# Where a routed expert layer begins: one-hots choice by choice, gather indices taken from the list itself, and a quarter of tile 0's gate and up ahead of tile 1's rows

## The chip, the core and the metric

The kernel runs on one core of a Trainium2 chip. The metric is the device time in microseconds of one execution, from the first to the last instruction and what lies around them; lower is better. The core has five engines with queues of their own: TensorE (PE), VectorE (DVE), ScalarE (ACT), GpSimd (POOL) and SyncE (SP), and 16 DMA engines which serve the transfers that any of them issue.

## The reference, cut to what matters

Eight sequences of 512 tokens with 512 features go through a cross attention (16 heads), are normalised, and then through a mixture of 8 experts, of which each token takes two:

```python
x = x + xattn(layernorm(x), ctx, ctx, Wq, bq, Wk, bk, Wv, bv, Wo, bo)
flat = layernorm(x).reshape(T, H)                       # T = 4096, H = 512
scores = softmax(flat @ router_weight.T + router_bias)  # 8 experts
topk_vals, topk_idx = top_k(scores, 2)
w = zeros((T, E)).at[arange(T)[:, None], topk_idx].set(topk_vals)
gu = einsum('th,ehf->tef', flat, gate_up_proj) + gate_up_bias      # 2 x 512 columns
gate, up = minimum(gu[..., :I], 7), clip(gu[..., I:], -7, 7)
down = einsum('tei,eih->teh', (up + 1) * gate * sigmoid(1.702 * gate), down_proj) + down_bias
x = x + einsum('teh,te->th', down, w)
```

## The kernel before

The program has three stages, each a block of its own, and at a block's end all five engines meet in a barrier before any of them starts on the next one.

**Attention** (`attention_stage`) works through 32 units of one sequence and four heads. A hand-written list `ORDER` gives every engine its work. At its end the last tokens get their router logits, and from them the best two experts (`hot[0]`, `hot[1]`; `hots` is both), their rank among the tokens of that expert (`place`), and their softmax weight (`share`). Tokens are handled in groups of 128-token tiles; groups 7 and 8 are the last five tiles. After `share` SP stores the weights behind the rows of the normalised input: row r of `xln_dram` holds 512 features and 8 weights. The store counts on the semaphore `w_stored`.

**Routing** (`routing_stage`) makes the work list. The experts' loads are cut into 39 tiles of 256 tokens. DVE works out each tile's expert (`tile_expert`, `tile_changed`); these two, marked "tiles", are what SP waits for before `first_loads`, which issues the weights of the first two tiles: twice 2 MB for gate and up (`raw_g`) and 1 MB for down (`raw_d`). The places of the first 27 tiles of tokens were written to DRAM earlier (`token_list`); those of the last five are put in by matmuls with one-hots: `at_hot` (place within a column, 128 wide) and `col_hot` (column of the list, 78 wide) for both choices s, into `list_ps`, and then the earlier list is added by `choose`. The result is `token_of`, 78 columns of 128 token numbers, two columns a tile.

**Experts** (`expert_stage`) handles the 39 tiles. For each tile POOL gathers 2 x 128 rows by indirect DMA (`fetch`), PE transposes them into `t_ps` (`turn_rows`), ACT and DVE split the result into a high and a low part (`row_hi`, `row_lo`), PE does gate and up in four parts f (`gate_up`, 24 matmuls a part, three passes of high and low), ACT and DVE the activation, PE the down product, and the sum goes back into `out` by gather, add and scatter. The weights are split into high and low in the same way, when a tile's expert differs from that of two tiles before (`gate_up_hi`, `gate_up_lo`). `fetch(0)` waits for all weight stores:

```python
e.wait_ge(w_stored, 16 * weights_stored)
fetch(0)
fetch(1)
fetch_sums(0)
```

Of the kernel before, what the change touches and what calls it, by code (L numbers as in the profile page):

```python
# [5 lines left out]
ALU = mybir.AluOpType  # L6
# [8 lines left out]
P = 128  # L15
# [53 lines left out]
def attention_stage(nc, x, ctx_t, w_t, bq, bk, bv, bo, router_wt, router_b, out, xln_dram, w_rows, w_stored, token_list, listed, route, ident):  # L69
# [8 lines left out]
    iota, token, base, before, ones_b, hot, ranks = (route[n] for n in ("iota", "token", "base", "before", "ones_b", "hot", "ranks"))  # L78

# [5 lines left out]

    weights_of = lambda g: slots_of(g) if g < groups[-1] else slice(SLOTS, SLOTS + 2)

    with ExitStack() as ctx:
# [54 lines left out]
        hots = sb("hots", [P, SLOTS, E], BF16)  # L143
        expo = sb("expo", [P, SLOTS, E])
        weight = sb("weight", [P, SLOTS + 2, E])
        exp_sum = sb("exp_sum", [P, SLOTS])
        inv_sum = sb("inv_sum", [P, SLOTS])
# [17 lines left out]
        def step(s):  # L165
# [537 lines left out]
        def on_dve(e):  # L703
# [136 lines left out]
            def share(g):  # L840
                slots, n = slots_of(g), GROUPS[g][1]
                e.wait_ge(softened.sem, softened[g])
                if g in groups[1:-1]:
                    e.wait_ge(w_stored, 16 * g)
                then(e.tensor_reduce(exp_sum[:, slots], expo[:, slots, :], AX.X, ALU.add))
                then(e.tensor_tensor(weight[:, weights_of(g), :], expo[:, slots, :], hots[:, slots, :], ALU.mult))
# [3 lines left out]
                e.tensor_tensor(weight[:, weights_of(g), :], weight[:, weights_of(g), :], inv_sum[:, slots].unsqueeze(2).to_broadcast([P, n, E]),  # L850
# [149 lines left out]
        def on_sp(e):  # L1000
# [63 lines left out]
            for kind, *what in ORDER:  # L1064
# [16 lines left out]
                elif kind == "share":  # L1081
                    g, = what
                    e.wait_ge(weight_made.sem, weight_made[g])
                    e.dma_start(w_rows[:, tiles_of(g), :], weight[:, weights_of(g), :]).then_inc(w_stored, 16)
# [12 lines left out]
def routing_stage(nc, route, token_list, listed, tile_hot, tile_expert, tile_changed, token_of, n_tiles, groups, first_loads):  # L1097
# [12 lines left out]
    KT = TOP_K * left  # L1110

    with ExitStack() as ctx:
# [11 lines left out]
        expert_f = sb("expert_f", [P, n_tiles])  # L1124
        changed_f = sb("changed_f", [P, n_tiles])
# [15 lines left out]
        at_hot = sb("at_hot", [P, KT, P])  # L1141
# [22 lines left out]
        def on_dve(e):  # L1164
# [8 lines left out]
            def last():  # L1173
# [23 lines left out]
            then(e.tensor_tensor(tile_hot[:, :, 0, :], iota[:, 0:E].unsqueeze(1).to_broadcast([P, n_tiles, E]),  # L1197
                                 expert_f[:, :].unsqueeze(2).to_broadcast([P, n_tiles, E]), ALU.is_equal))
# [649 lines left out]
```

## Time and profile before

| | |
|---|---|
| median of 3 runs | 1750.2 us (1749.93 to 1752.56) |
| the profiled execution, its own time | 1748.89 us |
| its span in the trace | 1747.2 us |
| mean granted TensorE clock | 0.969 of 2.4 GHz |
| TensorE matmuls busy | 1621.0 us, 93% of the span |
| TensorE weight loads busy | 1189.2 us, 68% |
| VectorE / ScalarE / GpSimd busy | 1278.3 / 659.2 / 856.5 us |

The profiled execution's own time is 1.69 us above its span, for what lies around the instructions. A busy share is a mean over the whole span: attention ends at about 990 us, routing runs from there to about 1010 us, and the experts take the rest. Times in the rows below are microseconds from the span's start.

### The profile page before, as it was taken

What the parts mean: (1) busy time and instruction counts of PE and PEld (TensorE: products, weight loads), DVE (VectorE), ACT (ScalarE), POOL (GpSimd) and SP (SyncE); (2) the same over time, 40 slices, a digit from 0 to 9 for tenths busy, and PEclk for the clock granted to TensorE, in tenths of its full rate; (3) what the DMA queues carried; (4) which work ended last, traced back from release to release, by engine and by line L of the source; (5) the groups of instructions that cost most, each with busy time, mean ns of one, the idle gap of its engine ahead of it and who ended that gap; (6) DMA issues with size and microseconds to landing.
All of it is one profiled execution on the core that took longest, in us unless ns stands there. A gap on an engine that the chain in (4) does not pass through costs nothing. (4 is left out here: it accounts for less than half of the span.)

```text
span 1747.2 us, 30307 instructions
## 1 busy us (share of the span) xinstructions
PE 1621.0 (93%) x9614; PEld 1189.2 (68%) x9614; DVE 1278.3 (73%) x2426; ACT 659.2 (38%) x1273; POOL 856.5 (49%) x677
## 2 busy tenths in 40 slices
PE   5889999999999999999997479999999999999995
PEld 3555555555555555555543369999999998999994
DVE  3675777878778777787785567777878688777873
ACT  3354544545445445444442142223332233223320
POOL 4365656566666666666767223343333333334332
PEclk9999999999999999999999579999999999999998
DMA  6342332433433434343322442234453353324321
GB/s 216 84 121 68 107 110 81 122 92 94 119 96 94 120 79 135 85 112 80 92 67 38 104 167 74 86 98 159 164 170 92 99 199 119 101 84 154 98 86 60
DMA packets 101077, 188.99 MB, mean 108 GB/s; under 512 B 28208, under 2 KB 29616, under 8 KB 100912
## 3 DMA queue, kind: packets, MB, share of 16 engines
q1 hardware_dynamic: 79952, 124.25, 24.9%
q0 software_dynamic: 20960, 62.76, 11.3%
q8 instruction: 77, 1.26, 0.4%
q14 instruction: 88, 0.72, 0.2%
HBM read 204.32 MB, written 37.51 MB: 138 GB/s over the span
## 5 line engine op out<-in xcount | busy, mean ns | idle before, releaser
L769 DVE TENSOR_REDUCE negmax<-max_ps 128x2 f32<-128x1024 f32 x256 | 312.2, 1220 | 162.9 <-PE max_ps L526 162.4
L650 ACT ACTIVATE pt<-work 128x512 f32<-128x512 f32 x512 | 278.3, 594 | 249.6 <-PE work L538 234.9
L946 POOL TENSOR_TENSOR acc<-acc,pt 128x1024 f32<-128x1024 f32 x128 | 303.7, 2376 | 129.2 <-ACT pt L650 129.1
L1440 PE MATMUL gu_ps<-xgT_hi,wg_hi 128*128 128x256 f32 x1248 | 356.3, 285 | 0.0
L1440 PE MATMUL gu_ps<-xgT_hi,wg_lo 128*128 128x256 f32 x1248 | 352.7, 283 | 0.0
L1440 PE MATMUL gu_ps<-xgT_lo,wg_hi 128*128 128x256 f32 x1248 | 351.9, 282 | 0.0
L943 POOL TENSOR_TENSOR acc<-pt 128x1024 f32<-128x1024 f32 x64 | 153.1, 2394 | 197.7 <-PE work L558 129.6
L1701 POOL DMA_INDIRECT out<-acc,idx x78 | 77.3, 991 | 329.0 <-DVE acc L1595 323.1
L1440 PEld LDWEIGHTS gu_ps<-xgT_lo,wg_hi 128*128 128x128 f32 x1248 | 236.3, 189 | 0.1
L1440 PEld LDWEIGHTS gu_ps<-xgT_hi,wg_hi 128*128 128x128 f32 x1248 | 236.0, 189 | 0.1
L1440 PEld LDWEIGHTS gu_ps<-xgT_hi,wg_lo 128*128 128x128 f32 x1248 | 235.6, 189 | 0.0
L526 PE MATMUL max_ps<-ks,qs 96*128 96x512 f32 x512 | 200.5, 473 | 26.0 <-DVE negmax L769 12.7
L1507 ACT ACTIVATE sig<-gate 128x256 f32<-128x256 f32 x156 | 65.1, 418 | 341.5 <-DVE gate L1559 338.9
L538 PE MATMUL work<-qs,ks 98*128 98x512 f32 x512 | 169.2, 407 | 11.6 <-DVE q_lo L756 5.6
L526 PEld LDWEIGHTS max_ps<-ks,qs 96*128 96x128 f32 x512 | 88.6, 193 | 87.8 <-issue 54.1
L550 PE MATMUL o_ps<-pt,v 128*32 128x512 f32 x1024 | 138.3, 612 | 1.7 <-ACT pt L650 1.7
L1454 PE MATMUL d_ps<-wd_hi,hid_hi 128*128 128x512 f32 x312 | 124.9, 400 | 9.5 <-DVE acc L1592 7.8
L1696 POOL DMA_INDIRECT acc<-out,idx x78 | 80.8, 1036 | 102.8 <-DMA out<-acc,idx 90.5
L538 PEld LDWEIGHTS work<-qs,ks 98*128 98x128 f32 x512 | 96.9, 191 | 47.0 <-issue 11.7
L780 DVE RECIPROCAL inv<-inv 128x128 f32<-128x128 f32 x128 | 120.7, 943 | 7.5 <-issue 4.8
L493 PE MATMUL work<-xT,wq 128*128 128x512 f32 x256 | 126.0, 615 | 0.0
L1559 DVE TENSOR_SCALAR gate<-gu_ps,bg 128x256 f32<-128x256 f32 x156 | 75.4, 484 | 66.9 <-PE gu_ps L1440 56.3
(211 smaller groups left out, 2971.5 us busy)
## 6 DMA issues: line engine op xcount, KB each, us to landing
raw_g<-w_gate_up SPq DMA_DIRECT2D x39, 2048.0 KB
raw_d<-w_down SPq DMA_DIRECT2D x39, 1024.0 KB
ks<-k_hi SPq DMA_DIRECT2D x252, 64.0 KB
qs<-q_hi SPq DMA_DIRECT2D x252, 64.0 KB
bd<-b_down SPq DMA_DIRECT2D x39, 256.0 KB
x_in<-x SPq DMA_DIRECT2D x32, 256.0 KB, 3.2
ctxT_raw<-ctx_t SPq DMA_DIRECT2D x32, 256.0 KB, 4.0
x<-x SPq DMA_DIRECT2D x32, 256.0 KB, 2.9
```

The source lines that it names most:

```text
L493: ins = e.matmul(to[:, :], wq[:, k, cols], xT[:, k, :], start=(k == 0), stop=(k == C - 1))
L526: ins = e.matmul(max_ps[:, j, :], qs[i][0:3 * HD, h, t * P:(t + 1) * P], ks[i][0:3 * HD, h, :], start=True, stop=True)
L538: e.matmul(to[:, :], ks[i][0:3 * HD + 2, h, k * P:(k + 1) * P], qs[i][0:3 * HD + 2, h, :], start=True, stop=True).then_inc(exp_ready.sem, 1)
L550: ins = e.matmul(o_ps[u % 2][HD * h:HD * (h + 1), :], v[:, k, c * P + HD * h:c * P + HD * (h + 1)], pt[k % 2][:, h, :], start=(k == 0), st ...
L650: e.activation(pt[k % 2][:, h, :], in_work("exp", u, k, h)[:, :], ACT.Exp, scale=scale).then_inc(exped.sem, 1)
L769: e.tensor_reduce(negmax[:, u % 2, n:n + 2], max_ps[:, :, :], AX.X, ALU.max, negate=True).then_inc(maxed.sem, 1)
L780: e.reciprocal(inv[:, cols], inv[:, cols]).then_inc(inverted.sem, 1)
L943: e.tensor_tensor(acc[:, heads, :], pt[0][:, heads, :], pt[1][:, heads, :], ALU.add).then_inc(added.sem, 1)
L946: e.tensor_tensor(acc[:, heads, :], acc[:, heads, :], pt[k % 2][:, heads, :], ALU.add).then_inc(added.sem, 1)
L1440: ins = e.matmul(gu_ps[n % GU_BANKS][:, part, :], wg[s][pw][:, k, cols], xgT[s][px][:, k, :], start=(k == 0 and m == 0), stop=(k == KD - 1 ...
L1454: ins = e.matmul(d_ps[j][:, :], hid[s][px][:, k, j * P:(j + 1) * P], wd[s][pw][:, k, :], start=(k == 0 and m == 0), stop=(k == KF - 1 and ...
L1696: e.indirect_dma_start(out=acc[s][:, j, :], out_offset=None, in_=out_rows, in_offset=slot_rows(i, j)).then_inc(acc_in[s], 16)
```

## The change

It has four parts.

1. The weights (`share`) of the last two groups move out of attention: routing makes them in one go for the last five tiles (40 columns), between `choose` and `token_1` on DVE, and SP stores them with one DMA after `first_loads`. The `w_stored` count that `fetch(0)` waits for drops by one, since there is one store fewer.
2. In routing, the one-hot of the tiles' experts (`tile_hot`) moves from ahead of `tile_expert` to behind `choose`, and `at_hot` and `col_hot` are made for choice 0, multiplied, and then for choice 1, where before both were made at once.
3. The gathers and scatters of the experts take a column of `token_of` as index; the copy into `idx` and its semaphore are gone.
4. PE does part f = 0 of tile 0's gate and up before `turn_rows(1)`; ACT does `row_hi(1)` behind the down weights of tile 0 and half the gate and up weights of tile 1.

```diff
-                at(3, ("best", g + 1, 0), ("best", g + 1, 1), ("count", g + 1), ("soft", g + 1), ("rank", g + 1), ("share", g), ("place", g + 1), ("share", g + 1))
+                at(3, ("best", g + 1, 0), ("best", g + 1, 1), ("count", g + 1), ("soft", g + 1), ("rank", g + 1), ("place", g + 1))
...
+            for s in range(TOP_K):
+                then(e.tensor_tensor(at_hot[:, s, :, :], iota[:, :].unsqueeze(1).to_broadcast([P, left, P]),
+                                     at_f[:, s, :].unsqueeze(2).to_broadcast([P, left, P]), ALU.is_equal))
+                then(e.tensor_tensor(col_hot[:, s, :, :], iota[:, 0:SLOTS].unsqueeze(1).to_broadcast([P, left, SLOTS]),
+                                     col_f[:, s, :].unsqueeze(2).to_broadcast([P, left, SLOTS]), ALU.is_equal))
+                last()
+                then(e.tensor_tensor(col_hot[:, s, :, :], col_hot[:, s, :, :],
+                                     token[:, done_tiles:].unsqueeze(2).to_broadcast([P, left, SLOTS]), ALU.mult), ("late", s))
...
+            e.wait_ge(w_stored, 16 * (len(groups) - 2))
+            then(e.tensor_reduce(exp_sum[:, late], expo[:, late, :], AX.X, ALU.add))
+            then(e.tensor_tensor(weight[:, late, :], expo[:, late, :], hots[:, late, :], ALU.mult))
+            last()
+            then(e.reciprocal(inv_sum[:, late], exp_sum[:, late]))
+            last()
+            then(e.tensor_tensor(weight[:, late, :], weight[:, late, :], inv_sum[:, late].unsqueeze(2).to_broadcast([P, left, E]), ALU.mult), "weights")
             e.wait_ge(listed_late, 1)
...
             first_loads(e)
+            e.wait_ge(vec, at["weights"])
+            e.dma_start(w_rows[:, done_tiles:, :], route["weight"][:, late, :]).then_inc(w_stored, 16)
...
             turn_rows(0)
-            for i in range(-1, n_tiles):
+            gate_up(0, range(1))
+            turn_rows(1)
+            gate_up(0, range(1, KF))
+            for i in range(n_tiles):
...
-                e.tensor_copy(idx[i % IDX][:, :], token_of[:, place * SUB:(place + 1) * SUB]).then_inc(idx_made.sem, 1)
-                e.wait_ge(idx_made.sem, idx_made[i])
```

On SP, from the last stores of attention to the end of routing (`xln_dram<-weight` is a store of weights, 3, 2 or 5 tiles of 8 columns; `rows` is the earlier list). Before:

```order
L1046 DMA xln_dram<-x 128x512 [waits ln2_made] x2
L1084 DMA xln_dram<-weight 128x3x8 [waits weight_made]
L1084 DMA xln_dram<-weight 128x2x8 [waits weight_made]
L1089 UNCONDITIONAL_BRANCH [waits xln_stored2,x2_stored2,x2_stored1,xln_stored3,xln_stored1,x2_stored3,x2_stored0,xln_stored0]
L1316 UNCONDITIONAL_BRANCH [waits barrier_Pool_Activation_PE_DVE_SP_release]
L1308 DMA rows<-token_list 128x2x128 [waits listed]
...
L1325 DMA raw_d<-w_down 128x4x512
L1312 UNCONDITIONAL_BRANCH
```

and now:

```order
L1040 DMA xln_dram<-x 128x512 [waits ln2_made] x2
L1083 UNCONDITIONAL_BRANCH [waits xln_stored2,x2_stored2,x2_stored1,xln_stored3,xln_stored1,x2_stored3,x2_stored0,xln_stored0]
L1318 UNCONDITIONAL_BRANCH [waits barrier_Pool_Activation_PE_DVE_SP_release]
L1308 DMA rows<-token_list 128x2x128 [waits listed]
...
L1327 DMA raw_d<-w_down 128x4x512
L1312 DMA xln_dram<-weight 128x5x8 [waits tiles_vec]
L1314 UNCONDITIONAL_BRANCH
```

Two small stores have left the end of attention, and one stands behind the last of the four weight loads.

On POOL, at the start of the experts, before:

```order
L1682 COPY idx<-token_of 128x2 [waits w_stored]
L1685 DMA xg<-xln_dram,idx 128x520 [waits idx_made]
L1685 DMA xg<-xln_dram,idx 128x520
L1682 COPY idx<-token_of 128x2
L1685 DMA xg<-xln_dram,idx 128x520 [waits idx_made]
L1685 DMA xg<-xln_dram,idx 128x520
L1696 DMA acc<-out,idx 128x512 x2
L1682 COPY idx<-token_of 128x2 [waits w_made,turned]
```

and now:

```order
L1684 DMA xg<-xln_dram,token_of 128x520 [waits w_stored]
L1684 DMA xg<-xln_dram,token_of 128x520 x3
L1696 DMA acc<-out,token_of 128x512 x2
L1684 DMA xg<-xln_dram,token_of 128x520 [waits w_made,turned]
L1684 DMA xg<-xln_dram,token_of 128x520
L1684 DMA xg<-xln_dram,token_of 128x520 [waits w_made,turned]
```

The copies and the wait for them are gone; the first gather itself now waits for `w_stored`.

On PE, the first rows of the experts: transposes of tile 0 (`gathered0`), of tile 1 (`gathered1`) and the first matmuls of gate and up. Before:

```order
L1424 MATMUL t_ps<-ident,xg 128x128 [waits gathered0]
L1424 MATMUL t_ps<-ident,xg 128x128 x3
L1424 MATMUL t_ps<-ident,xg 128x128 [waits xgT_lo_made,gathered1]
L1424 MATMUL t_ps<-ident,xg 128x128 x3
L1424 MATMUL t_ps<-ident,xg 128x128 [waits xgT_lo_made,gathered1]
L1424 MATMUL t_ps<-ident,xg 128x128 x3
L1440 MATMUL gu_ps<-xgT_hi,wg_hi 128x256 [waits xgT_lo_made,wg_lo_made0]
```

and now:

```order
L1424 MATMUL t_ps<-ident,xg 128x128 [waits gathered0]
L1424 MATMUL t_ps<-ident,xg 128x128 x3
L1440 MATMUL gu_ps<-xgT_hi,wg_hi 128x256 [waits xgT_lo_made,wg_lo_made0]
L1440 MATMUL gu_ps<-xgT_lo,wg_hi 128x256
...
L1440 MATMUL gu_ps<-xgT_hi,wg_lo 128x256
L1424 MATMUL t_ps<-ident,xg 128x128 [waits xgT_lo_made,gathered1]
```

The 24 matmuls of part 0 stand ahead of the eight transposes of tile 1.

## Rows read from the trace of the kernel before

**Rows 1.** The page: shares of the chain that ended last, by engine

```profile
PE 38%; DVE 1%; issue 1%; DMA 1%; POOL 0%; ACT 0%; ACTq 0%; DVEq 0%; POOLq 0%
```

**Rows 2.** Waits of PE after 1023 us: total us, times, longest

```profile
PE d_ps L1454 <- DVE acc L1592: 7.8, 5, 2.7
PE d_ps L1454 <- DVE hid_lo L1574: 1.6, 1, 1.6
```

**Rows 3.** Timeline of PE where the experts start: start, length, work, idle before

```profile
1017.32 1.97 PE L1424 MATMUL t_ps<-ident,xg 128*128 128x128 f32 x8 [8.99 <-DMA xg<-xln_dram,idx]
1021.02 1.97 PE L1424 MATMUL t_ps<-ident,xg 128*128 128x128 f32 x8 [1.74 <-DMA xg<-xln_dram,idx]
1022.64 0.56 PE L1440 MATMUL gu_ps<-xgT_hi,wg_hi 128*128 128x256 f32 x1
```

**Rows 4.** Timeline of DVE where the experts start

```profile
1019.95 0.69 DVE L1551 TENSOR_TENSOR xgT_lo<-t_ps,xgT_hi 128x512 fp32r<-128x512 f32 x1 [0.16 <-ACT xgT_hi L1481]
...
1034.11 1.22 DVE L1405 TENSOR_TENSOR wg_lo<-raw_g,wg_hi 128x1024 fp32r<-128x1024 f32 x1
```

**Rows 5.** Timeline of POOL where the experts start

```profile
1010.53 0.18 POOL L1682 COPY idx<-token_of 128x2 int32<-128x2 int32 x1 [18.54 <-POOLq L1312]
1011.27 1.06 POOL L1685 DMA_INDIRECT xg<-xln_dram,idx  x1 [0.56 <-POOL idx L1682]
1012.63 1.02 POOL L1685 DMA_INDIRECT xg<-xln_dram,idx  x1 [0.31 <-issue]
...
1022.81 0.95 POOL L1685 DMA_INDIRECT xg<-xln_dram,idx  x1 [0.30 <-issue]
```

**Rows 6.** DMA queue totals, 995 to 1014.5 us: packets, MB, share

```profile
q1 hardware_dynamic: 2046, 6.19, 84.5%
```

**Rows 7.** DMA queue totals, 1014.75 to 1015 us

```profile
q0 software_dynamic: 15, 0.06, 67.0%
q1 hardware_dynamic: 93, 0.02, 41.6%
```

**Rows 8.** Timeline of SP: last stores of attention, list, first weight load

```profile
989.79 1.02 SPq L1084 DMA_DIRECT2D xln_dram<-weight  x2
991.55 0.36 SPq L1308 DMA_DIRECT2D rows<-token_list  x1
997.24 0.40 SPq L1325 DMA_DIRECT2D raw_g<-w_gate_up  x1
```

**Rows 9.** DMA issues, whole span: KB each, median us from issue to landing

```profile
xln_dram<-x SPq DMA_DIRECT2D x32, 256.0 KB, 3.3
...
qs<-m_hi SPq DMA_DIRECT2D x32, 8.0 KB, 1.8
...
bk_col<-bk SPq DMA_DIRECT2D x1, 2.0 KB, 10.3
```

**Rows 10.** Timeline of DVE at the end of attention

```profile
989.68 0.17 DVE L858 COPY ranks<-work 128x16 f32<-128x16 f32 x1
...
990.25 0.17 DVE L850 TENSOR_TENSOR weight<-weight,inv_sum 128x16 f32<-128x16 f32 x1
```

**Rows 11.** Timeline of DVE in routing

```profile
994.18 0.48 DVE L1197 TENSOR_TENSOR tile_hot<-iota_f,expert_f 128x312 bf16<-128x312 f32 x1
...
997.12 1.49 DVE L1228 TENSOR_TENSOR at_hot<-iota_f,at_f 128x1280 f32<-128x1280 f32 x1
998.53 0.96 DVE L1231 TENSOR_TENSOR col_hot<-iota_f,col_f 128x780 f32<-128x780 f32 x1
999.53 1.04 DVE L1235 TENSOR_TENSOR col_hot<-col_hot,consts 128x390 f32<-128x390 f32 x2
...
1005.60 0.24 DVE L1252 COPY token<-list_ps 128x78 f32<-128x78 f32 x1 [3.25 <-PE list_ps L1293]
```

**Rows 12.** Busy time by stretch: PE, PEld, DVE, ACT, POOL, PEclk, DMA share, GB/s

```profile
1024.00:1026.00 2.00, 2.00 (x12) 2.00 (x11) 0.00 (x0) 2.00 (x5) 0.00 (x0) 0.51 0.64 179
1026.00:1028.00 2.00, 2.00 (x18) 2.00 (x18) 1.22 (x2) 2.00 (x3) 0.00 (x0) 1.00 0.00 0
```

More of the change, by code:

```diff
@@ L78, in attention_stage @@
     iota, token, base, before, ones_b, hot, ranks = (route[n] for n in ("iota", "token", "base", "before", "ones_b", "hot", "ranks"))
+    expo, hots, weight, exp_sum, inv_sum = (route[n] for n in ("expo", "hots", "weight", "exp_sum", "inv_sum"))
     SLOTS = 2 * T
@@ L1249, in on_dve @@
                 then(e.tensor_scalar(choose[:, c, :], row_slot[:, :], number[:, 0:1], None, ALU.is_equal), "choose")
+            then(e.tensor_tensor(tile_hot[:, :, 0, :], iota[:, 0:E].unsqueeze(1).to_broadcast([P, n_tiles, E]),
+                                 expert_f[:, :].unsqueeze(2).to_broadcast([P, n_tiles, E]), ALU.is_equal))
+            expo, hots, weight, exp_sum, inv_sum = (route[n] for n in ("expo", "hots", "weight", "exp_sum", "inv_sum"))
+            e.wait_ge(w_stored, 16 * (len(groups) - 2))
[5 more added lines that the diff above has]
+            then(e.tensor_tensor(weight[:, late, :], weight[:, late, :], inv_sum[:, late].unsqueeze(2).to_broadcast([P, left, E]), ALU.mult), "weights")
             e.wait_ge(listed_late, 1)
@@ L1288, in on_pe @@
                 for t in range(left):
-                    e.matmul(list_ps[:, :], at_hot[:, s * left + t, :], col_hot[:, s, t, :], start=(s == 0 and t == 0), stop=False)
+                    e.matmul(list_ps[:, :], at_hot[:, s, t, :], col_hot[:, s, t, :], start=(s == 0 and t == 0), stop=False)
             e.wait_ge(rows_in, 16)
@@ L1360, in expert_stage @@
         bu1 = [sb(f"bu1{s}", [P, KF]) for s in range(2)]
-        idx = [sb(f"idx{s}", [P, SUB], I32) for s in range(IDX)]
         xg = [sb(f"xg{s}", [P, SUB, DX]) for s in range(2)]
@@ L1531, in on_act @@
                         gate_up_hi(1, k, changed)
+                    row_hi(1)
                 if i + 2 < n_tiles:
@@ L1687, in slot_rows @@
             def slot_rows(i, j):
-                return bass.IndirectOffsetOnAxis(ap=idx[i % IDX][:, j:j + 1].bitcast(U32), axis=0)
+                column = in_list(i, n_tiles) * SUB + j
+                return bass.IndirectOffsetOnAxis(ap=token_of[:, column:column + 1].bitcast(U32), axis=0)
             def fetch_sums(i):
@@ L1779, in build @@
         route["hot"] = [sb(f"hot{i}", [P, 2 * T, E]) for i in range(TOP_K)]
+        route["expo"] = sb("expo", [P, 2 * T, E])
+        route["hots"] = sb("hots", [P, 2 * T, E], BF16)
+        route["weight"] = sb("weight", [P, 2 * T, E])
+        route["exp_sum"] = sb("exp_sum", [P, 2 * T])
+        route["inv_sum"] = sb("inv_sum", [P, 2 * T])
         route["ranks"] = sb("ranks", [P, 2 * T, E])
@@ L1811, in build @@
         groups = route_groups(NT, T)
-        routing_stage(nc, route, token_list, listed, tile_hot, tile_expert, tile_changed, token_of, n_tiles, groups, first_loads)
-        expert_stage(nc, raw, s_raw, xln_dram, w_stored, len(groups), out, w_gate_up, w_down, b_gate_up, b_down, tile_hot, tile_expert, tile_changed, token_of, ident, n_tiles)
+        routing_stage(nc, route, w_rows, w_stored, token_list, listed, tile_hot, tile_expert, tile_changed, token_of, n_tiles, groups, first_loads)
+        expert_stage(nc, raw, s_raw, xln_dram, w_stored, len(groups) - 1, out, w_gate_up, w_down, b_gate_up, b_down, tile_hot, tile_expert, tile_changed, token_of, ident, n_tiles)
 _INS = ["x", "ctx_t", "wq_t", "bq", "wk_t", "bk", "wv_t", "bv", "wo_t", "bo", "router_wt", "router_b",
```

48 lines of the change are left out of this document (14 added, 34 removed).

## The prediction

> **What bounds the kernel now.** The chain of work that ended last comes first: 38% of the span is PE's (each line's share is of the pieces that could be followed back), and no other engine has more than 1% [rows 1]. After 1023 us PE is held only 7.8 + 1.6 us in all, by DVE [rows 2]. So from the first matmul of gate and up PE runs through, and anything done in the 39 expert tiles apart from PE's own work is hidden. What the change can move is the moment at which PE starts to run through; everything behind it shifts by the same amount. The timeline of PE dates that moment at 1021.02 us: the transposes of tile 0 run at 1017.32, PE then idles 1.74 us, takes tile 1's transposes at 1021.02, and gate and up follow at 1022.64 without a gap [rows 3].
>
> What was late at that moment? Tile 1's rows. Tile 0's low part was ready at 1019.95 + 0.69 = 1020.64 us [rows 4], so matmuls could have begun 0.4 us before tile 1's rows were there. One step back, PE waited 8.99 us for tile 0's rows [rows 3], whose second gather POOL issued at 1012.63 [rows 5]: 4.7 us from issue to PE's start. The queue totals say why so long. Up to 1014.5 us the SP queue had moved 6.19 MB, nearly the 6.29 MB of the first weight loads, and the answer for that stretch has no line for POOL's queue at all [rows 6], though its first gather was issued at 1011.27 and the second at 1012.63 [rows 5]. From 1014.75 to 1015 POOL's queue holds 67% of the engines and SP's moves only 93 small packets [rows 7]. The weight loads thus drained at about 1014.75 us, and the gathers moved only then. Tile 0's rows are tied to the drain, not to POOL.
>
> **The change, part by part.** *End of attention.* SP issued its two weight stores at 989.79 to 990.81 us and the barrier let it go to the list at 991.55 [rows 8]. DVE's last instruction ended at 990.25 + 0.17 = 990.42; without the shares its last one is the rank copy, which ends at 989.68 + 0.17 = 989.85 [rows 10]. If SP's issues held the barrier, it opens 0.96 us earlier by those ends, and up to 1.5 us earlier if the eight waits that SP does behind the stores (estimated at 0.3 us) go with them, and DVE's copy no longer stands behind the shares of group 7. I take 1.5, bounds 0.6 (DVE's end alone) and 1.6.
>
> *Routing, DVE.* `tile_hot` leaves the chain to "tiles": from its start at 994.18, 0.48 us and a 0.04 us step, 0.52 in all [rows 11]. So the weight loads begin 1.5 + 0.52 = 2.0 us earlier (bounds 1.1 and 2.1), and so does their drain: 1014.75 becomes 1012.75 us. The one-hots: choice 0 is ready for PE at 999.53 + 0.52 = 1000.05 us, after 1.41 us of `at_hot` and 1.0 of `col_hot` for both choices; with half of each first, 1.2 us less. From there PE's 24 matmuls, and not DVE, fill the time to 1005.60 (5.5 us). The moved `tile_hot` (0.48) and the new weights (four small instructions of about 0.2) come to 1.3 us between `choose` and `token_1`, where DVE idles 3.25 us [rows 11]; PE starting 1.2 earlier leaves it about 2.0, so they are hidden. Routing would end 1.5 + 0.52 + 1.0 to 1.2 = 3.1 us earlier, and POOL would be free at 1010.53 - 3.1 = 1007.4 us [rows 5].
>
> *The store behind the loads.* This is the term that decides. SP now issues the weights' store behind four weight loads, at about 1002 us, ten microseconds before they drain, and `fetch(0)` waits for its landing. Does a small transfer overtake large ones on SP's queue? At the start of the program 2 KB of bias, issued behind megabytes of weights, took 10.3 us to land, while 8 KB took a median 1.8 us elsewhere [rows 9]. It does not overtake. So the store's data moves at 1012.75 us and takes 0.4 us (640 packets). Of the small transfer's 1.8 us I give half, as an estimate, to the way from issue to first data, which the wait in the queue covers here, and half, 0.9, to landing. The stores into `xln_dram` took 3.3 us for 256 KB; less 0.9 for issue and 0.7 for the data (the weight loads moved 6.19 MB in some 16 us, 0.38 MB a microsecond [rows 6]) that leaves 1.7. I take 0.9, since 20 KB are nearer to the 8, and keep 0 and 1.7 as ends. `w_stored` is complete at 1012.75 + 0.4 + 0.9 = 1014.05 us, 2.8 us later than the first gather's issue before.
>
> *The gathers.* Without `idx` the first starts 0.1 us behind that, the second 1.06 + 0.3 later, at 1015.5 [rows 5]. From there to PE's start it took 4.7 us before, among bias loads of 256 KB. The next pair, with the queue free, was issued at 1022.81 and its data had ended by 1026 [rows 5, 12]: at most 3.2 us, and 0.9 to land as above. I take 4.25 between 4.1 and 4.7. Tile 0's rows then reach PE at 1019.75 us, 2.4 later than now. From PE's first transpose to the low part it was 1020.64 - 1017.32 = 3.3 us [rows 3, 4], 3.4 with the step to PE: part 0 starts at 1023.15. A column of `token_of` as index costs a gather nothing that I count: the list's scatters take columns in the same way.
>
> *Part 0 ahead of tile 1's rows.* PE now runs through from part 0 on, and tile 1's transposes, moved behind it, find their rows. The amount of PE work is unchanged, so the shift is 1023.15 - 1021.02 = +2.1 us. This part alone would have brought 0.4 us. Behind it ACT takes `row_hi(1)` later, and what is late next is DVE's last low part of tile 1's gate and up, at 1034.11 + 1.22 = 1035.33 before [rows 4]; it moves by about 1.4 us, the start of tile 1's gate and up on PE by 2.1, so it stays hidden. Were it not, each microsecond would come on top.
>
> *The steady state.* `idx` saved on POOL (0.74 us from copy to gather [rows 5]) in each tile meets no wait of PE for gathers; the 9.4 us that PE waits there are DVE's [rows 2]. Nothing.
>
> *The clock.* It is granted at half (1.2 GHz) until just before 1026 us and at full after [rows 12]. I let the stretch at 1.2 GHz move along with PE's start. If it is counted by matmuls alone, it ended 3.3 us behind the first of them (1022.64 [rows 3]), and now part 0 starts the count at once: 1.6 us less at half speed, 0.7 us gained. The Trainium skill says this in "TensorE: Matmul & The Clock Gate", Part 4: a PE-mode transpose does not count as PE-busy in the same way. By that rule the sum would be +1.4 us; no row of this trace tells the two apart, so it is an end of the range only.
>
> **Sum.** PE's run no longer waits for tile 1's rows, -0.4; tile 0's rows come 2.4 later and the step to part 0 costs 0.1: +2.1 us, 1021.02 to 1023.15. Span 1747.2 becomes 1749.3, the profiled execution's own time 1748.89 becomes 1751.0; the median, 1.3 above that execution, 1750.2 becomes 1752.3 us. Its ends: drain -0.1 or +0.9, landing -0.9 or +0.8, gathers -0.15 or +0.45, clock -0.7; all at once that is +0.3 to +4.3, and the case's own range is +0.5 to +3.5, 1750.7 to 1753.7.
>
> **Rivals.** *Not held (faster side, small).* The store lands early, and the gathers alone hang on the drain: rows arrive 2.0 us earlier, and part 0 starts at 1017.32 - 2.0 + 3.4 = 1018.7, -2.3 us: 1747.9. For it: the one moves into the chip and the other out of it; against it the 10.3 us [rows 9].
>
> *Not held, and sharing (faster).* If the gathers also got a share of the DMA engines, POOL free at 1007.4, second gather at 1008.8, rows at 1013.5, part 0 at 1016.9: -4.1 us, 1746.1. Against it the missing line of POOL's queue [rows 6]. The Trainium skill has the rule for it, in "DMA: Bandwidth & Descriptors", Queues, rings and completion order: each DMA engine takes the rings it has work for in turn, packet by packet. By that rule the gathers would have moved in the stretch in which the trace has none.
>
> *Slower.* The store's landing, one mechanism: each microsecond that it lands later is a microsecond of time. At 1.7 us of landing and a drain only 1.1 us earlier, `w_stored` is complete at 1015.75 and the time is +3.8: 1754.0. It decides from 1015.5 us on (+3.5). For it: writes into these rows land slowly [rows 9].
>
> *No change at all*, gains and hold-up cancelling within 0.5 us, is the low end of the forecast's range.
>
> **How the numbers follow.** A measurement of this kernel tells about 0.2%, 3.5 us, from no change. Forecast (held by the queue, +0.5 to +3.5): 0.68. Not held: 0.12. Not held, sharing: 0.06. Slower by over 3.5: 0.14. So faster 0.07, same 0.79, slower 0.14. The range reaches from the second case to just into the slower one, 1747.0 to 1754.5 us.
>
> **What would show it.** Right: the barrier opens near 990.0, `raw_g` is issued near 995.2, the one store stands behind the loads, POOL idles from 1007.4 to about 1014 and PE's first transpose comes near 1019.7, part 0 near 1023.2. Wrong: a gather issued before 1012; POOL's packets among the weight loads' (then the sharing case); a wait of PE ahead of tile 1's gate and up near 1038.

## The result: the start as forecast, and every expert tile 0.6 us shorter

| | before | changed |
|---|---|---|
| median | 1750.07 us (1747.85 to 1752.56, 4 runs) | 1736.26 us (1730.35 to 1738.46, 4 runs) |
| profiled execution, its span | 1748.89, 1747.2 us | 1730.35, 1728.6 us |
| TensorE matmuls busy | 1621.0 us | 1596.3 us |
| mean granted TensorE clock | 0.969 | 0.971 |

The ratio is 0.9917, interval 0.9896 to 0.9937: 0.8% faster, 14 us, where the forecast was 2.1 us slower. The time lies outside the range and outside every rival.

The place that the prediction worked on came out nearly to the tenth. The timeline of the changed kernel where the experts start (start, length, engine, work, idle before):

```profile
990.12 0.17 PE L1285 MATMUL count_ps<-before,ones_b 128*128 128x8 bf16 x1 [0.54 <-PEq L1083]
...
995.26 0.41 SPq L1327 DMA_DIRECT2D raw_g<-w_gate_up  x1
...
1001.71 0.47 SPq L1312 DMA_DIRECT2D xln_dram<-weight  x1
...
1014.70 1.03 POOL L1684 DMA_INDIRECT xg<-xln_dram,token_of  x1 [24.17 <-DMA xln_dram<-weight]
1016.04 0.96 POOL L1684 DMA_INDIRECT xg<-xln_dram,token_of  x1 [0.30 <-issue]
...
1020.03 1.97 PE L1424 MATMUL t_ps<-ident,xg 128*128 128x128 f32 x8 [14.77 <-DMA xg<-xln_dram,token_of]
1027.97 1.03 PE L1424 MATMUL t_ps<-ident,xg 128*128 128x128 f32 x8
1037.02 1.03 PE L1424 MATMUL t_ps<-ident,xg 128*128 128x128 f32 x8
```

Against [rows 8]: the weight loads begin 1.98 us earlier (forecast 2.0). That two absolute times can be set side by side at all is luck: up to DVE's last rank copy both executions took the same time (989.68 and 989.62 us), while in the other kernels' traces this copy stands anywhere from 989.4 to 999.2. What the change does there is the way from this copy to `count_ps`, 1.90 us before and 0.50 now. The store stands behind the loads, and POOL waits for its landing until 1014.70 (forecast 1014.05), not for work of its own. Against [rows 3, 5]: tile 0's rows reach PE at 1020.03 (forecast 1019.75), part 0 starts at 1023.5 (forecast 1023.15). Tile 2's transposes, at 1035.70 us before, stand at 1037.02: 1.32 us later.

From there on the sign turns. Tile 38's transposes ran at 1683.76 us before and run at 1668.04 now, 15.7 us earlier. Nothing that PE waits for has gone; the waits of PE after 1024 us in the changed kernel (us in total, times, longest) are larger than those of [rows 2]:

```profile
PE d_ps L1454 <- DVE acc L1596: 11.1, 10, 3.1
PE d_ps L1454 <- DVE hid_lo L1578: 1.6, 1, 1.6
PE gu_ps L1440 <- DVE xgT_lo L1555: 1.5, 1, 1.5
```

What has changed is the pace of matmuls that the change does not touch. The groups of gate and up (count, busy us, mean ns of one, idle before), first of before:

```profile
L1440 PE MATMUL gu_ps<-xgT_hi,wg_hi 128*128 128x256 f32 x1248 | 356.3, 285 | 0.0
L1440 PE MATMUL gu_ps<-xgT_hi,wg_lo 128*128 128x256 f32 x1248 | 352.7, 283 | 0.0
L1440 PE MATMUL gu_ps<-xgT_lo,wg_hi 128*128 128x256 f32 x1248 | 351.9, 282 | 0.0
```

and of the changed kernel:

```profile
L1440 PE MATMUL gu_ps<-xgT_hi,wg_hi 128*128 128x256 f32 x1248 | 349.1, 280 | 1.5 <-DVE xgT_lo L1555 1.5
L1440 PE MATMUL gu_ps<-xgT_lo,wg_hi 128*128 128x256 f32 x1248 | 345.6, 277 | 0.0
L1440 PE MATMUL gu_ps<-xgT_hi,wg_lo 128*128 128x256 f32 x1248 | 345.4, 277 | 0.0
```

The listed length of one falls by 6 ns of 283, and these lengths overlap. The distance from start to start is what PE's time is made of. The timeline of before, in the middle of a tile:

```profile
1200.03 0.28 PE L1440 MATMUL gu_ps<-xgT_lo,wg_hi 128*128 128x256 f32 x1
1200.15 0.28 PE L1440 MATMUL gu_ps<-xgT_hi,wg_lo 128*128 128x256 f32 x1
1200.27 0.28 PE L1440 MATMUL gu_ps<-xgT_hi,wg_hi 128*128 128x256 f32 x1
1200.39 0.28 PE L1440 MATMUL gu_ps<-xgT_lo,wg_hi 128*128 128x256 f32 x1
```

and of the changed kernel:

```profile
1300.03 0.28 PE L1440 MATMUL gu_ps<-xgT_hi,wg_lo 128*128 128x256 f32 x1
1300.14 0.28 PE L1440 MATMUL gu_ps<-xgT_hi,wg_hi 128*128 128x256 f32 x1
1300.25 0.28 PE L1440 MATMUL gu_ps<-xgT_lo,wg_hi 128*128 128x256 f32 x1
1300.37 0.28 PE L1440 MATMUL gu_ps<-xgT_hi,wg_lo 128*128 128x256 f32 x1
```

Both at the full clock. Over a whole tile the spacing (mean of all starts in the tile, and of these the median tile) is 119.6 ns before and 114.4 ns now in gate and up, 232.2 and 228.7 ns in down; before, eight of the even tiles had 120.9 in gate and up. A tile has 96 and 24 of them: 96 x 5.2 + 24 x 3.5 = 583 ns, and the tiles' starts say the same: 17.85 us apart before, 17.27 us now (medians). The 36 tiles from 2 to 38 brought 17.0 us, not 21: 3.2 of the missing 4 are PE's waits at `d_ps` for DVE, 5.3 us in these tiles now and 2.1 before, so a quicker PE meets DVE more often. The profiled execution of the changed kernel is also the quickest of its four; the medians are 14 us apart.

### The profile page after: what moved, and what is told of

Same layout as the page of the kernel before. It is cut to its first block and busy times, and to the rows that moved or that the text cites. A ratio compares the mean times of both kernels' runs of the same rounds, so it can differ in the third digit from the quotient of the medians.

```text
span 1728.6 us, 30264 instructions
## 1 busy us (share of the span) xinstructions
PE 1596.3 (92%) x9614; PEld 1167.6 (68%) x9614; DVE 1274.5 (74%) x2424; ACT 659.2 (38%) x1273; POOL 837.3 (48%) x638
## 5 line engine op out<-in xcount | busy, mean ns | idle before, releaser
L1440 PE MATMUL gu_ps<-xgT_hi,wg_hi 128*128 128x256 f32 x1248 | 349.1, 280 | 1.5 <-DVE xgT_lo L1555 1.5
L1440 PE MATMUL gu_ps<-xgT_lo,wg_hi 128*128 128x256 f32 x1248 | 345.6, 277 | 0.0
L1440 PE MATMUL gu_ps<-xgT_hi,wg_lo 128*128 128x256 f32 x1248 | 345.4, 277 | 0.0
L1701 POOL DMA_INDIRECT out<-acc,token_of x78 | 77.4, 992 | 324.2 <-DVE acc L1599 318.4
L1696 POOL DMA_INDIRECT acc<-out,token_of x78 | 81.9, 1050 | 104.3 <-DMA out<-acc,token_of 91.9
L1454 PE MATMUL d_ps<-wd_lo,hid_hi 128*128 128x512 f32 x312 | 124.2, 398 | 0.0
```

Of the source, the lines that this page charges most:

```text
L1440: ins = e.matmul(gu_ps[n % GU_BANKS][:, part, :], wg[s][pw][:, k, cols], xgT[s][px][:, k, :], start=(k == 0 and m == 0), stop=(k == KD - 1 ...
L1454: ins = e.matmul(d_ps[j][:, :], hid[s][px][:, k, j * P:(j + 1) * P], wd[s][pw][:, k, :], start=(k == 0 and m == 0), stop=(k == KF - 1 and ...
L1696: e.indirect_dma_start(out=acc[s][:, j, :], out_offset=None, in_=out_rows, in_offset=slot_rows(i, j)).then_inc(acc_in[s], 16)
```

## The theories

What in the change reaches into the steady state? Three things were put against each other. *Place*: the change moves `expo`, `hots`, `weight`, `exp_sum` and `inv_sum` out of attention into the part of SBUF that lives all through, and drops `idx`; every tensor of the experts therefore lies elsewhere, `wg` and `wd` 704 bytes and `xgT` and `hid` 512 bytes higher in each partition. *Copies*: POOL no longer copies `idx` in each tile. *Order*: tile 0's part ahead of tile 1's rows, and ACT's new order, let the tiles fall into another rhythm.

## The experiments

**a_moved** and **d_no_copy**: the kernel before with one thing of the change each. In a_moved it is the places alone; the notes behind # are not in the kernel.

```diff
+        sb("shift_all", [P, 176])      # a_moved: 704 unused bytes ahead of tile_hot
...
-        idx = [sb(f"idx{s}", [P, SUB], I32) for s in range(IDX)]
         xg = [sb(f"xg{s}", [P, SUB, DX]) for s in range(2)]
...
+        idx = [sb(f"idx{s}", [P, SUB], I32) for s in range(IDX)]   # a_moved: behind hid
```

```diff
-                e.tensor_copy(idx[i % IDX][:, :], token_of[:, place * SUB:(place + 1) * SUB]).then_inc(idx_made.sem, 1)
-                e.wait_ge(idx_made.sem, idx_made[i])
...
-                return bass.IndirectOffsetOnAxis(ap=idx[i % IDX][:, j:j + 1].bitcast(U32), axis=0)
+                column = in_list(i, n_tiles) * SUB + j
+                return bass.IndirectOffsetOnAxis(ap=token_of[:, column:column + 1].bitcast(U32), axis=0)
```

> The kernel before, with nothing changed but where the experts' tensors lie in SBUF: an unused tensor of 704 bytes a partition ahead of them and the idx tensors behind them put every one at the address it has in the changed kernel. Theory PLACE (the pitch of the gate and up matmuls, 120.0 ns before and 113.3 ns after, comes from the addresses): the pitch is 113.3 ns, a tile takes about 17.3 us where it took 17.85, and the time falls by about 18 to 21 us, ratio 0.988 to 0.990. Theory COPIES (POOL's index copies and the semaphore behind them slow PE): pitch 120.0, ratio 1.000. Theory ORDER (part 0 ahead of tile 1's rows, or the earlier start, sets another phase between PE and DVE): pitch 120.0, ratio 1.000.

> The kernel before with only the index copies and their semaphore taken out; the idx tensors stay allocated, so no address changes. COPIES: pitch 113.3 ns and a ratio of 0.988 to 0.990. PLACE and ORDER: pitch 120.0 ns and a ratio of 1.000, at most 0.7 us less at the start, if that.

Measured: a_moved 1734.86 us (1731.43 to 1743.97), ratio 0.9913 (0.9886 to 0.994), spacing 114.4 and 228.7 ns, a tile in 17.27 us. d_no_copy 1754.03 us, ratio 1.0012 (0.9992 to 1.0031), a tile in 17.85 us. Unused bytes alone, with every instruction of before in its old order, give the whole gain. The copies give nothing.

**b_moved_back**: the changed kernel with two unused pieces, which put every expert tensor 1024 bytes above its address of before.

```diff
+        sb("shift_all", [P, 80])
...
+        sb("shift_rows", [P, 48])
         xg = [sb(f"xg{s}", [P, SUB, DX]) for s in range(2)]
```

> The changed kernel, with the experts' tensors each exactly 1024 bytes above their address in the kernel before (two unused tensors of 320 and 192 bytes a partition), all else kept. PLACE: the pitch goes back to 120.0 ns, and only the start's shift is left, which the trace of the changed kernel shows as +1.3 us at tile 2's transposes: ratio to the kernel before 1.000 to 1.002. COPIES and ORDER: pitch 113.3, ratio about 0.990 as the changed kernel.

Measured: 1755.17 us (1750.34 to 1759.48, 12 runs), ratio 1.0016 (1.0002 to 1.0031), that is +2.8 us (0.4 to 5.4). Its groups of gate and up are those of before:

```profile
L1441 PE MATMUL gu_ps<-xgT_hi,wg_hi 128*128 128x256 f32 x1248 | 356.3, 286 | 1.5 <-DVE xgT_lo L1556 1.5
L1441 PE MATMUL gu_ps<-xgT_hi,wg_lo 128*128 128x256 f32 x1248 | 352.6, 283 | 0.0
```

This is the change that the diff shows, with the addresses taken out of it; the forecast of +2.1 us belongs to this kernel, and the interval holds it. *Order* falls with it: the new order is all there, and a tile takes 17.85 us.

**c_store_act**: the changed kernel, but ACT's queue and not SP's carries the weights' store.

```diff
-            e.wait_ge(vec, at["weights"])
-            e.dma_start(w_rows[:, done_tiles:, :], route["weight"][:, late, :]).then_inc(w_stored, 16)
+        def on_act(e):
+            e.wait_ge(vec, at["weights"])
+            e.dma_start(w_rows[:, done_tiles:, :], route["weight"][:, late, :]).then_inc(w_stored, 16)
```

> The changed kernel, with the store of the last five tiles' weights issued by ACT, not behind SP's weight loads. If the store's place in SP's queue is what holds the gathers, as I forecast, the first gather is issued near 1007.5 us and not at 1014.7, its data still waits until the weight loads drain near 1012.8, PE's first transpose comes near 1015.5 to 1017.5 and not at 1020.0, and the time is 2.5 to 4.5 us below the changed kernel's. If small transfers of another queue wait as long, no change. PLACE, COPIES and ORDER all expect a pitch of 113.3 ns here.

Measured: 1740.72 us (1737.36 to 1747.78, 7 runs), ratio 0.994 (0.992 to 0.9961). The end of attention moves by some microseconds from run to run (`count_ps` ran at 990.1 us in the changed kernel's profile and at 998.4 in this one), so positions are counted from `count_ps`. The timeline of this kernel:

```profile
1009.97 0.40 ACTq L1314 DMA_DIRECT2D xln_dram<-weight  x1
...
1020.69 1.66 POOL L1687 DMA_INDIRECT xg<-xln_dram,token_of  x1 [21.90 <-DMA xln_dram<-weight]
```

The store had a queue of its own with nothing ahead of it, and POOL still went on only 10.7 us behind its issue; in SP's queue it was 13.0. The first gather stood 22.3 us behind `count_ps` (24.6 in the changed kernel), tile 0's rows 28.8 (29.9). My expectation, a gather near 1007.5 us, 17.4 behind `count_ps`, is refuted. The queue totals of this kernel from 1014 to 1019 us (packets, MB, share) say what happened:

```profile
q1 hardware_dynamic: 551, 1.99, 97.6%
q10 hardware_dynamic: 551, 0.02, 6.2%
```

q1 is SP's queue with the weight loads, q10 is ACT's with the store: for each packet of the loads one of the store moved. The Trainium skill says in "DMA: Bandwidth & Descriptors", Queues, rings and completion order, that an engine takes its rings in turn, packet by packet; the trace agrees. But the store is 656 packets of about 32 bytes, and the packet of the loads between two of them has 3.6 KB on average, so its packets took from 1013.8 to 1020.0 us. Nor did they begin at once: between the issue at 1009.97 and 1013.8 there is none, and no run shows why. So the store did not wait for the drain here, it was drawn out. POOL's gathers had no such turns in [rows 6]: the first moved 3.4 us behind its issue, as the loads ended, where in the changed kernel, with the loads gone, it took 1.7.

**e_two_places** and **f_two_more**: the changed kernel with unused columns that give the tensors of even and of odd tiles different places. Modulo 128 bytes, e has `wg` and `wd` at 96 (even) and 32 (odd), with `xgT` and `hid` at 32; f has 0 and 64, with 0.

```diff
+        def placed(name, shape, s, at):
+            over = (at - -(-nc.sbuf_base // 32) * 32) % 128
+            if over:
+                sb(f"{name}_space{s}", [P, over // 4])
+            return pair(name, shape, s)
+        wg = [placed("wg", [P, KD, F2], s, (96, 32)[s]) for s in range(2)]
```

> The changed kernel with unused space put in so that the residues of the addresses modulo 128 bytes differ between even and odd tiles: even tiles have gate and up weights (and down weights) at 96, odd tiles at 32; the moving rows xgT and the hidden values hid lie at 32 for both. In the kernel before it was 96 for the weights and 96 for xgT and hid (slow, 119.6 ns), in the changed one 32 and 96 (fast, 114.4). Theory PAIR (PE is slowed when both operands of a matmul start at the same residue): even tiles 114.4 ns in gate and up and about 228.8 in down, odd tiles 119.6 and 232.2. Theory OWN (the weights' residue alone, 96 slow and 32 fast): even tiles 119.6 and 232.2, odd tiles 114.4 and 228.8.

> As the run before, with xgT and hid at residue 0 modulo 128, even tiles' weights at 0 and odd tiles' at 64. PAIR: even tiles slow (119.6 ns), odd tiles fast (114.4). OWN says nothing of 0 and 64 by itself; if what counts is a start on a boundary of 64 bytes, both are alike and perhaps faster than 114.4; if it is a boundary of 128, even tiles alone are.

PAIR and OWN are the two rules that the expectations set against each other. Measured, one execution each: e 1745.54 us, f 1751.4 us. Gate and up: e 118.7 in even tiles (one of them, tile 34, 114.4) and 119.6 in odd ones; f 119.6 in even tiles and mostly 114.2 in odd ones. Down: e 233.0 and 227.8; f 227.8 and 233.3. One slot of a kernel can be quick in one product and slow in the other, so it is nothing that the kernel has as a whole. Both rules fail: PAIR asked for 114.4 and 228.8 in e's even tiles, OWN for 114.4 and 228.8 in its odd ones, and neither pair of numbers came. I first laid a tile's numbers to the wrong parity in gate and up, and took from these runs that the weights' own place modulo 128 decides. **h_rows_at_96** was made to try that: f with `xgT` and `hid` at 96.

> The changed kernel, with unused columns ahead of the experts' tensors so that (address in a partition, modulo 128 bytes) the weights wg and wd stand at 0 for even tiles and at 64 for odd ones, and the rows xgT and hid at 96 for all. If the weights' own place decides (in the first or the second half of 128 bytes), even tiles have gate and up spaced 114 ns and down 228 ns (a tile in some 17.25 us) and odd ones 119.6 and 232 (17.85 us), whatever the rows' place; span between 1742 and 1750 us. If the distance between the two operands decides, even tiles (distance 96 - 0, seen nowhere before; the changed kernel has 64 and is quick, the kernel before has 0 and is slow) can come out either way, and odd ones (distance 32) as well: then the pattern of the run with rows at 0 (even quick, odd slow) need not return.

Measured: 1753.32 us; gate and up 119.2 and 119.6, down 233.9 and 233.9 ns. Only `xgT` and `hid` (and what lies between them) had moved, and all that had been quick in f was slow. The weights' own place does not decide.

**g_loads_later** and **i_down_later** ask what the store behind the loads costs. In g, SP loads only tile 0's weights ahead of the store; in i, the gate and up weights of both tiles, and the down weights later.

```diff
-            for i in range(2):
-                load_gate_bias(i)
-                load_down_bias(i)
+            load_gate_bias(0)
+            e.wait_ge(gathered[0], turn(0) * 16 * SUB)
+            load_gate_up(e, raw_g[1], w_gate_up, tile_expert, tile_changed, 1, raw_g_in[1])
+            load_down(e, raw_d[1], w_down, tile_expert, tile_changed, 1, raw_d_in[1])
...
-            for s in range(2):
+            for s in range(1):
```

> The changed kernel, with the addresses left alone. SP loads only tile 0's weights (3 MB) ahead of the weights' store; tile 1's 3 MB are issued in the expert stage, after tile 0's rows have landed. If the queue ahead of the store and of the gathers is what held tile 0's rows, as I forecast, the weight loads drain near 1004.5 us, the store has landed when POOL is free at 1007.4, PE's first transpose comes near 1011.5 and not at 1020.0, measured from the same end of attention, and the time is 6 to 8.5 us below the changed kernel's; tile 1's weights are then late by at most 1 us. If it was the latency of store and gathers themselves, less than 2 us are gained.

> The changed kernel, but SP issues only the gate and up weights of tiles 0 and 1 (4 MB) ahead of the weights' store, and the down weights of both in the expert stage, once tile 0's rows have landed. Addresses as in the changed kernel. If the store and the first gathers wait for what stands ahead of them in SP's queue, 4.2 MB drain some 11 us behind the first load, near 1006 us, before POOL is free (about 1008 in a run whose attention ends at 990); the first gather then starts as in the run with tile 1's loads late (18 us behind count_ps), tile 0's rows are there at 23 us instead of 30, and tile 1's gate and up weights are no longer late: tile 2's transposes at 38 to 40 us behind count_ps instead of 47, the median 6 to 8 us below the changed kernel, 1728 to 1731, ratio 0.986 to 0.989. If tile 0's down weights come late in turn, its down part waits and gives some of it back: PE would show a wait at d_ps of tile 0. If the order of the loads does not matter, 1736, ratio 0.992.

Measured: g 1731.96 us (1730.68 to 1732.86, 6 runs), ratio 0.9899 (0.9876 to 0.9921); i 1740.26 us (1737.04 to 1742.82), ratio 0.9917 (0.9898 to 0.9936). The timeline of g, whose `count_ps` ran at 991.23:

```profile
1009.28 1.03 POOL L1684 DMA_INDIRECT xg<-xln_dram,token_of  x1 [17.64 <-POOLq L1314]
...
1014.35 1.97 PE L1424 MATMUL t_ps<-ident,xg 128*128 128x128 f32 x8 [7.96 <-DMA xg<-xln_dram,token_of]
...
1027.42 2.01 ACT L1399 ACTIVATE wg_hi<-raw_g 128x1024 fp32r<-128x1024 f32 x2 [8.39 <-DMA raw_g<-w_gate_up]
...
1033.72 1.27 PE L1424 MATMUL t_ps<-ident,xg 128*128 128x128 f32 x8 [2.33 <-DVE xgT_lo L1555]
```

With 3 MB ahead of the store, POOL waits for its own work only and tile 0's rows come 23.1 us behind `count_ps`, not 29.9. Tile 2's transposes gain 4.4 us. But ACT then waits 8.4 us for tile 1's weights, and from tile 2 to tile 3 it takes 22.0 us where the changed kernel takes 17.8: all is given back. In i the same, with the down weights late (2.9 us gained at tile 2, 4.5 lost behind it). The bytes must come in either way, and what stands last in the queue is late. g is the quickest kernel here, but its interval overlaps that of the changed one.

**j_bursts**: PE alone, on zeros, with the whole computation left out: bursts at the very addresses of the kernels above, and 64 pairs of places modulo 256.

```python
for at in PLACES:
    mark()
    for f in range(4):
        gate_up(at, f)
    mark()
    down(at)
for at in GRID + BITS:
    mark(); gate_up(at, 0); gate_up(at, 1)
```

> Leaves out the whole computation: the output is filled with zeros, and PE multiplies zeros in bursts, with nothing running beside it. First ten bursts of one tile's gate and up (96 matmuls of 256 columns) and down (24 matmuls of 512 columns), at exactly the addresses that the tensors of even and of odd tiles have in the kernel before, the changed kernel and the runs with two places, two more and rows at 96; then 64 bursts of 48 gate-and-up matmuls, with the weights' address (the stationary operand) and the rows' (the moving one) each at 0, 32, ... 224 modulo 256; then 12 with one of the two moved by 4 to 2048 bytes. A burst of one matmul marks the joints. If the operands' addresses alone set the spacing, the first ten bursts repeat what the kernels showed: gate and up 119.6, 119.6, 114.4, 114.4, 119.6, 118.7, 114.2, 119.5, 119.6, 119.2 ns, and the 64 show which bits of which operand decide. If it takes other engines' work on the same memory (ACT, DVE and POOL read and write there in the kernels) all bursts are equal, 113 to 115 ns.

The timeline of PE (start, length of the group, count); a burst's spacing is the next start less its own, by the count:

```profile
86.39 11.55 PE L84 MATMUL gu_ps<-big 128*128 128x256 f32 x96
97.77 0.28 PE L96 MATMUL mark_ps<-big 128*128 128x256 f32 x1
...
120.82 11.07 PE L84 MATMUL gu_ps<-big 128*128 128x256 f32 x96
131.72 0.28 PE L96 MATMUL mark_ps<-big 128*128 128x256 f32 x1
```

The first is at the addresses of before, (97.77 - 86.39) / 96 = 118.5 ns; the second at those of the changed kernel, (131.72 - 120.82) / 96 = 113.5 ns. Nothing else ran, so no other engine and no DMA has part in it. Nine of the ten bursts of gate and up fall on the side on which the kernels had them (before 118.5 and 118.8, changed 113.5 and 113.5, e 113.5 and 118.5, f 118.8 and 113.3, h 118.2 and 117.4); the tenth is e's even tiles, 113.5 alone and 118.7 in the kernel. Down agrees in all ten.

**k_grid**: the same with one pair of operands repeated 24 times, 16 by 16 places modulo 512, in two orders, and 8 by 8 for down.

```python
for a, b in BURSTS:      # a, b: 0, 32, ... 480
    mark()
    for n in range(24):
        e.matmul(gu_ps[...], view(69632 + a, P), view(188416 + b, FTOK), ...)
```

> Leaves out the whole computation, as the bursts did, with nothing running beside PE. Here a burst is 24 times the same pair of operands (no walk over k and parts). The stationary operand stands at 0, 32, ... 480 behind a multiple of 512, the moving one (256 columns) likewise: 256 bursts, and all of them once more in the other order; then 64 bursts with 512 moving columns, modulo 256. If the distance between the operands decides, the table is constant along its diagonals, and the quick diagonals (113.5 ns, where the others have 117 to 120) are those that the walk showed, 192 or 448 and perhaps 64 and 320. If each operand's own address decides, the table has quick rows and columns. If neither, quick cells lie scattered, the same in both orders; and if they differ between the two orders, it is no matter of addresses but of the instructions' place in the stream.

A quarter of the first order (ns from start to start; rows: the stationary operand's place, columns: the moving one's):

```
        0    32    64    96   128   160   192   224
  0 120.0 117.9 117.9 120.0 118.7 118.3 114.2 117.9
 32 118.3 119.2 117.1 117.9 120.0 118.3 117.1 114.2
 64 113.3 118.3 119.6 117.1 117.9 119.6 118.7 118.7
 96 118.7 114.2 118.3 119.6 117.9 117.9 120.0 118.7
128 118.3 118.7 113.8 118.3 120.0 117.1 117.5 120.0
160 119.6 118.8 117.5 114.6 118.3 120.0 116.7 117.5
192 117.5 119.6 118.3 117.5 117.9 118.3 120.0 116.7
224 116.7 117.5 120.4 119.6 118.8 114.2 117.9 119.6
```

It reads along its diagonals. Moved on by 256 bytes in one operand, all but two at most of these 64 cells come out the same. With the distance taken as moving less stationary, modulo 256: of 64 cells at a distance of 192, 50 are quick (113.3 to 114.6 ns); at 64, 8 of 64; at the other six distances none of 384 (116.7 to 120.4). For down the quick distances are 0 (all 8 cells, 227.1 to 229.2 ns) and 64 (5 of 8 at 230.0 or less); the rest have 232.1 to 234.6. Of the 32 places at 192, 18 are quick in both orders, 14 in one of the two, and none in neither; at 64 it is 2, 4 and 26. So no place at 192 is slow by itself: what ran before the burst counts too.

Laid beside the whole kernels, the distances (worked out from the tensors' addresses) order nearly all that was measured:

| kernel, tiles | gate and up: distance, ns | down: distance, ns |
|---|---|---|
| before, b, d: all | 128, 119.6 (even tiles up to 120.9) | 128, 232.2 |
| changed, a: all | 192, 114.4 | 64, 228.7 |
| e even | 192, **118.7** | 192, 233.0 |
| e odd | 128, 119.6 | 0, 227.8 |
| f even | 128, 119.6 | 0, 227.8 |
| f odd | 64, mostly 114.2 | 64, 233.3 |
| h even | 224, 119.2 | 160, 233.9 |
| h odd | 160, 119.6 | 224, 233.9 |

Only e's even tiles are slow at a quick distance (all but tile 34, which is quick at the same addresses); 64 goes either way, as in the table of bursts.

**l_rows_by_64** and **m_by_192**, in whole kernels: l is before with 64 unused bytes ahead of `xgT` and 64 ahead of `hid`; m is the changed kernel with both operands elsewhere and the distance kept.

```diff
+        sb("rows_space", [P, 16])
         xgT = [pair("xgT", [P, KD, FTOK], s) for s in range(2)]
...
+        sb("hid_space", [P, 16])
         hid = [pair("hid", [P, KF, FTOK], s) for s in range(2)]
```

> The kernel before with two unused pieces of 64 bytes, one ahead of xgT and one ahead of hid, and nothing else: no weight moves. The distance from the stationary operand to the moving one, modulo 256 bytes, was 128 in gate and up and 128 in down; it is 192 and 0 here, for tiles of both parities. If that distance decides, as the two runs of bursts say, gate and up go to 113.5 to 114.5 ns a matmul and down to 228, a tile from 17.85 to 17.25 us, and the median to 1731 to 1736 us, ratio 0.989 to 0.992, as in the changed kernel. If the weights' own place decides, nothing changes: 119.6, 232.2, 17.85 us, ratio 1.000. Against the first stand the even tiles of the run with two places, which had the same addresses modulo 256 (weights at 96, rows at 32) and 118.7 ns beside 113.5 in their burst: if whatever else runs in a tile undoes the quick spacing there, gate and up come to 118.7, down to 228, a tile to 17.65, and the median to 1742 to 1746.

> The changed kernel with unused columns so that the distance stays 192 modulo 256 in gate and up while both operands move (weights and rows at 64 and 0 for even tiles, 128 and 64 for odd ones; 32 and 224 in the changed kernel), and is 0 in down in place of 64. If the distance decides, all tiles stay quick: 113.5 to 114.5 ns, down 228 in place of 228.7, a tile in 17.25 us, median and ratio as the changed kernel's, 1735 and 0.990 to 0.993. If the operands' own places modulo 128 decide, as the whole-kernel runs alone would allow, odd tiles (weights at 0, rows at 64) are new and even ones, with weights at 64, slow: 119.5 ns, at least 9 us more, 1744 or above.

Measured: l 1738.52 us (1735.17 to 1743.07, 6 runs), ratio 0.992 (0.9895 to 0.9945); m 1737.43 us (1733.84 to 1742.82), ratio 0.9922 (0.9898 to 0.9947). m is quick in all tiles: 114.3 to 114.7 and 227.4 to 227.8 ns, with weights at 64 and at 0 modulo 128, where h had both slow. The groups of l stand between the two kinds:

```profile
L1442 PE MATMUL gu_ps<-xgT_hi,wg_hi 128*128 128x256 f32 x1248 | 351.8, 282 | 0.0
L1442 PE MATMUL gu_ps<-xgT_lo,wg_hi 128*128 128x256 f32 x1248 | 348.4, 279 | 0.0
```

By tiles: from tile 4 on the even ones have 114.4 ns and the odd ones 118.7, at the same distance of 192 and the same places modulo 256; down has 227.4 to 227.8 in nearly all. So 128 bytes of nothing make the kernel before 0.8% faster, and no weight has moved. Neither theory's number is met: the distance is what makes the quick pace possible, and something else decides at times whether it is taken.

## Why the prediction was wrong

- **What bounds the kernel**: right, PE runs through from the first part of gate and up. But this makes the time per matmul the one number that counts, 39 tiles times 120 of them, and I took it as given.
- **End of attention and routing**: right. Loads 1.98 us earlier (2.0); POOL's stream was free when the store landed.
- **The store behind the loads**: right in size, 1014.70 against 1014.05 us. That a store does not overtake in its own queue was right. In a queue of its own it took turns with the loads and still came only 2.3 us earlier (c_store_act), so the place in SP's queue is not the whole price.
- **Gathers and part 0**: right, 1020.03 against 1019.75 and 1023.5 against 1023.15.
- **The clock**: I let the stretch at 1.2 GHz move along with PE's start and kept 0.7 us of gain as an end. The rows of the changed kernel by stretch (PE, PEld, DVE, ACT, POOL busy, granted clock, DMA share, GB/s):

```profile
1024.00:1026.00 2.00, 2.00 (x12) 2.00 (x11) 0.21 (x1) 2.00 (x4) 1.49 (x2) 0.50 0.17 39
1026.00:1028.00 2.00, 2.00 (x15) 2.00 (x15) 2.00 (x2) 0.60 (x1) 0.41 (x1) 0.74 0.70 206
```

  The level changes from 1.2 to 2.4 GHz near 1027.0 us. PE had then run through for 3.5 us, and for 4.9 us before (1021.02 to just before 1026), so 0.7 us is gained as in that end. b_moved_back shows such a gain without the quicker matmuls; there the level rises 2.9 us after part 0 begins, which gives back 1.0 us. Counted from `count_ps`, tile 2's transposes stand at 46.98 us there and at 44.12 before; less the 1.46 us by which `count_ps` comes earlier, that is +1.4 us, the sum of that end, and not +2.1. But the moment moves from execution to execution: in the nine traces with the new order the level rises 2.9 to 6.1 us behind the first matmul of gate and up (5.9 in m_by_192), in the four with the old order 2.7 to 3.3. So these gains are in part luck. The Trainium skill says in "TensorE: Matmul & The Clock Gate", Part 4, that a transpose does not count as busy in the same way; with such a spread no run here settles whether that is the reason.
- **The step that failed** is in the part on part 0 and the steady state: "The amount of PE work is unchanged, so the shift is 1023.15 - 1021.02 = +2.1 us", and "Nothing" for the steady state. The number of matmuls is unchanged, their time is not: 0.58 us less in a tile, 17.0 us by tile 38. The term that was missing is the allocation. The diff moves five tensors and drops one, and I read it as who computes what and when, never as what lies where. a_moved has this term alone (ratio 0.9913), b_moved_back all the rest (1.0016); their product, 0.993, lies within the measured interval.
- **The rivals**: not held, sharing and slower all argued over the start, and none of them came. What the sharing one says of the gathers is not borne out by [rows 6]; for a store in ACT's queue sharing is what c_store_act shows, at 551 packets to 551, and it helped little. None had a term for the pace of the matmuls.

What stays open: why a burst or a tile at a distance of 192 is sometimes slow (14 of 64 cells, each quick in the other order; the odd tiles of l; e's even tiles, quick by themselves), and the mechanism in the chip. The runs give the pattern, not its reason. The Trainium skill has lines of 16 bytes in SBUF ("SBUF — State Buffer", Specifications); by those alone all places here, multiples of 32, would be alike, and they are not.

## What to carry to other kernels

When PE runs through, compare the start-to-start spacing of its matmuls before and after, not only its waits: a change that adds, drops or moves any tensor moves all that are allocated behind it. Here the distance in SBUF between the moving and the stationary operand, modulo 256 bytes, was worth some 5 ns in each matmul, with 256 and with 512 moving columns, though the quick distance was not the same (192 and 0); try a few paddings of 32 to 224 bytes between the two. And to know what an edit does by itself, put the addresses back with unused columns, and measure that.

## What was not expected of the hardware

- The spacing of fp32r matmuls depends on the two operands' distance: 256 columns in 113.3 to 114.6 ns in 50 of 64 bursts at 192 modulo 256, 116.7 to 120.4 ns at distances other than 64 and 192; 512 columns in 227.1 to 229.2 at 0, 232.1 to 234.6 at others than 0 and 64. It is about 5 ns a matmul in both, and shows with PE running alone.
- At half clock it does not show: 213.3 ns a matmul in tile 0's first part in both kernels.
- A 20 KB store of 656 small packets, on a queue of its own, took turns packet by packet with 6.3 MB of another queue's loads (551 and 551 in 5 us), and POOL could go on only 10.7 us behind its issue.
